# A preactivated 7x7 convolution: banks marked once, merged statistics, a new prologue, and 32 of 128 partitions normalised by GpSimd

## The reference

```
def _gn(v, G=32, eps=1e-05):            # one group per channel
    g = v.reshape(B_, G, C_ // G, H_, W_)
    return ((g - mean(g)) / sqrt(var(g) + eps)).reshape(v.shape)

kern = construct_kernel(weight, P)      # (32, 32, 7, 7): 9 points a channel, bilinear
out  = conv(x_normalised, kern, stride 1, padding 3) + bias
x    = x + out
```

## Time and profile before

| | |
|---|---|
| median of 3 runs | 374.69 us (374.63 to 374.84) |
| profiled execution | 374.54 us, of which its span is 372.7 us |
| PE busy | 330.5 us (89%) |
| DVE busy | 301.7 us (81%) |
| ACT busy | 245.4 us (66%) |
| POOL busy | 99.1 us (27%), nearly all of it the issue of transfers |
| mean granted TensorE clock | 0.954 |

### The profile page before, as it was taken

How to read it: one execution, slowest core, us unless ns; L and a number is a source line. 1 busy time by engine, 2 the same in 40 slices (tenths; PEclk the granted TensorE clock), 3 DMA queues, 4 the chain that set the end, 5 groups by cost and what they waited for, 6 DMA issues and landing times.

```text
span 372.7 us, 9633 instructions
## 1 busy us (share of the span) xinstructions
PE 330.5 (89%) x3426; PEld 206.7 (55%) x3426; DVE 301.7 (81%) x418; ACT 245.4 (66%) x361; POOL 99.1 (27%) x222
## 2 busy tenths in 40 slices
PE   2811799999999999999999999999999999999990
PEld 2600455666656665666655665666556665656560
DVE  6139599989898988989898989899898989898331
ACT  2297786868586785958585858678695858380110
POOL 6002405041424232240504142423224050415000
PEclk9965599999999999999999999999999999999996
DMA  8832608989899989899998989997999976676704
GB/s 144 147 60 57 181 2 183 182 199 204 187 198 194 204 165 216 152 215 173 204 194 189 200 175 197 179 217 150 210 165 215 161 185 138 158 168 164 163 1 86
DMA packets 128424, 61.30 MB, mean 164 GB/s; under 512 B 122228, under 2 KB 122260, under 8 KB 128404
## 3 DMA queue, kind: packets, MB, share of 16 engines
q1 hardware_dynamic: 117108, 25.34, 42.3%
q0 software_dynamic: 9216, 35.30, 41.6%
q10 hardware_dynamic: 2080, 0.40, 0.6%
HBM read 12.88 MB, written 12.85 MB: 69 GB/s over the span
## 4 chain that ended last, share of the span: by engine, by line
PE 60%; DVE 12%; issue 10%; ACT 1%; DVEq 0%
PE ps_s L713 19%; PE ps_x L713 18%; PE ps_eo L713 17%; DVE part L451 4%; DVE xs L447 3%; PE ps_y L696 2%; PE ps_x L696 2%; PE ps_y L713 2%; DVE result L451 2%; PE ps_stat L665 1%; ACT std L297 1%; DVE rtmp L420 1%; DVE rinv L414 1%; DVE scale L425 1%; DVE rtmp L418 1%
## 5 line engine op out<-in xcount | busy, mean ns | idle before, releaser
L642 POOL DMA_DIRECT2D xb<-xs x192 | 92.9, 491 | 244.0 <-ACT xs L322 129.7
L713 PE MATMUL ps_s<-xs,w 128*64 128x392 f16 (+1 forms) x576 | 108.6, 339 | 7.2 <-DVE part L451 5.9
L713 PE MATMUL ps_s<-xb,w 128*64 128x392 f16 (+1 forms) x576 | 108.4, 339 | 6.3 <-DMA xb<-xs 6.3
L713 PEld LDWEIGHTS ps_s<-xs,w 128*64 128x64 f16 x576 | 61.9, 111 | 37.7 <-issue 10.4
L309 ACT ACTIVATE xn<-xraw,offset,scale 96x784 f32<-96x784 f32 x64 | 67.2, 1049 | 19.6 <-DVE offset L427 18.3
L713 PE MATMUL ps_x<-xs,w 128*64 128x392 f16 x384 | 71.2, 342 | 0.0
L713 PE MATMUL ps_x<-xb,w 128*64 128x392 f16 x384 | 71.2, 342 | 0.0
L713 PE MATMUL ps_eo<-xb,w 128*64 128x392 f16 (+1 forms) x384 | 70.7, 342 | 0.0
L713 PE MATMUL ps_eo<-xs,w 128*64 128x392 f16 (+1 forms) x384 | 70.7, 342 | 0.0
L713 PEld LDWEIGHTS ps_s<-xb,w 128*64 128x64 f16 x576 | 61.7, 111 | 8.6 <-DMA xb<-xs 6.7
L713 PEld LDWEIGHTS ps_eo<-xs,w 128*64 128x64 f16 x384 | 41.7, 112 | 27.2 <-issue 6.5
(11 more groups left out here) (87 smaller groups left out, 437.6 us busy)
## 6 DMA issues: line engine op xcount, KB each, us to landing
xb<-xs POOLq DMA_DIRECT2D x96, 180.0 KB, 4.3
xb<-xs POOLq DMA_DIRECT2D x96, 179.0 KB, 4.8
out<-result SPq DMA_DIRECT2D x128, 98.0 KB, 3.4
xraw<-x SPq DMA_DIRECT2D x124, 98.0 KB, 5.8
xraw<-x ACTq DMA_DIRECT2D x4, 98.0 KB, 3.6
wnat<-L_conv_weight SPq DMA_DIRECT2D x1, 36.0 KB, 1.9
pts<-L_conv_P ACTq DMA_DIRECT2D x2, 1.1 KB, 1.9
biascol<-L_conv_bias SPq DMA_DIRECT2D x1, 0.5 KB
```

Of the source, the lines that this page charges most:

```text
L642: pool.dma_start(dst[32 * g:32 * g + 32, 0:run - QP * past], src[32 * f:32 * f + 32, QP * past:run]).then_inc(shifted[par][b], DMA)
L713: last = pe.matmul(into[p:p + HALF, :, :, 0:wide], w[:, n // 2, s, q, t, :], xs_or_xb[:, par, s, n % 2, :, t:t + ROWS, q:q + wide], start= ...
```

## The change

PE no longer zeroes the banks in each unit: eight matmuls of zeros at the start (and two more ahead of unit 0) mark `ps_y` and `ps_x`, and after that no stream into them starts afresh. `seed` waits for the merge that freed the bank instead. The two statistics of a unit share one tile `moments` and one pair of half-width folds per unit, ahead of stream 4 (`both_moments`): variance of unit u+2 and mean of unit u+3. `eo`, `part` and the merges run in the order (column, phase), so that `result` is written with a step of two values and the two banks of a pair are read in turn. DVE's step has a new order: B0, B1, second differences, outs_0, B2, outs_1, var, B3, rstd, mean, B4, outs_2, B5, outs_3, outs_4. ACT's step puts the squares behind B0 and the sums ahead of B2. POOL takes the two normalisations of partitions 96 to 127 over from ACT, ahead of the second third's transfers; DVE and ACT wait for both parts, and so does SP's load. The prologue has another order: POOL issues the transfers of the points and weights, a small identity is built first, the mean of unit 0 is folded within the filter's build, DVE scales the filter, and PE does both statistics of unit 1 (and the mean of unit 2) ahead of unit 0's first stream. The last unit's stores are split over SP and ACT.

```diff
-NORMS = 4
+NORMS = 2
...
-        eo = sb("eo", [128, 2, N], fp32)
-        part = sb("part", [128, 2, 2, N], fp32)
+        eo = sb("eo", [128, N, 2], fp32)
+        part = sb("part", [128, 2, N, 2], fp32)
...
         def two_phases(flat, k):
-            return flat.rearrange("p (n k) -> p k n", k=4)[:, k::2, :]
+            return flat.rearrange("p (n k) -> p n k", k=4)[:, :, k::2]
...
+        def last_store(queue, first):
+            queue.wait_ge(combined, OUTS * UNITS)
+            for m in range(PER):
+                for g in (first, first + 2):
+                    put(queue, UNITS - 1, (UNITS - 1) % 2, m, g)
...
                     sp.wait_ge(seeded, 2 * u + 2)
+                    sp.wait_ge(last_group_normalised, NORMS * u + NORMS)
                     load(u + RING, h)
...  ACT, normalise
-                    for a, b, slot in ((0, 96, 1), (96, 128, 0)):
...
+                    act.activation(xn[0:96, r % 2, SLOTS * m + 1:SLOTS * m + 1 + ROWS, PAD:PAD + SIDE],
...  ACT, step
                 if nxt:
                     high(u + 1, a, *BATCHES[0], first=first)
-                    high(u + 1, a, *BATCHES[1], first=first)
-                middle(u, first)
-                seed(u, h, 0)
                 if stats:
                     squares(u + 2, (h + 2) % RING)
                 if nxt:
+                    high(u + 1, a, *BATCHES[1], first=first)
+                middle(u, first)
+                seed(u, h, 0, first)
+                if early:
+                    sums(u + 3, (h + 3) % RING, nth)
+                if nxt:
                     for batch in BATCHES[2:]:
                         high(u + 1, a, *batch, first=first)
-                seed(u, h, 1)
-                if early:
-                    sums(u + 3, (h + 3) % RING, nth)
+                seed(u, h, 1, first)
...  POOL
+            def normalise(u):
+                pool.wait_ge(newton, NEWTON * (u + 1))
+                if u > 1:
+                    pool.wait_ge(differenced, DIFFS * (u - 1))
+                    pool.wait_ge(hi_ready, NS * (u - 1))
+                    pool.wait_ge(lo_ready, NS * (u - 1))
+                for m in range(PER):
+                    pool.tensor_scalar(xn[96:128, u % 2, SLOTS * m:SLOTS * m + ROWS, PAD:PAD + SIDE],
+                                       image(u % RING, m)[96:128, :].rearrange("p (n w) -> p n w", w=SIDE),
+                                       scale[96:128, m:m + 1], offset[96:128, m:m + 1], ALU.mult, ALU.add
+                                       ).then_inc(last_group_normalised, 1)
...
             for u in range(UNITS):
-                for b in range(THIRDS):
-                    shift(u, u % 2, b)
+                shift(u, u % 2, 0)
+                if u == 0:
+                    shift(u, u % 2, 1)
+                if u + 1 < UNITS:
+                    normalise(u + 1)
+                if u:
+                    shift(u, u % 2, 1)
+                shift(u, u % 2, 2)
...  PE
+            def fold_columns(a, b):
+                for p in (0, HALF):
+                    last = pe.matmul(ps_stat[p:p + HALF, a:b], fold[:, p:p + HALF], moments[:, a:b],
+                                     start=True, stop=True)
+                last.then_inc(folded, 1)
...
-            def start(pair):
-                for k in range(2):
-                    last = pe.matmul(pair[:, k, 0:N], zeros[:, 0:128], zeros[:, 128:128 + N], start=True, stop=False)
-                last.then_inc(started, 1)
...
+            mean(1)
+            both_moments(1)
...
                     if s == 4:
-                        if not first:
-                            pe.wait_ge(combined, OUTS * (u - 1) + 5)
-                        start(ps_y)
+                        if stats:
+                            both_moments(u + 2, early)
                         pe.wait_ge(seeded, 2 * u + 1)
```

More of the change, by code:

```diff
@@ L386, in _ @@
             filter_high(4)
-            high(0, 0, *BATCHES[4], first=True)
-            high(0, 0, *BATCHES[5], first=True)
+            for batch in BATCHES[2:]:
+                high(0, 0, *batch, first=True)
+            squares(1, 1)
+            sums(2, 2, 0)
             root(1)
-            sums(2, 2, 0)
             normalise(1, 1, first=True)
@@ L637, in shift @@
                 dst = xb[:, par, 3 * b:3 * b + 3].rearrange("p s a m n q -> p (s a m n q)")
-                for g in range(GROUPS):
+                for g in (0, 2, 1, 3):
                     past, k = divmod(WINDOW[g] + 2, GROUPS)
@@ L650, in _ @@
         @block.tensor
         def _(pe):
+            pe.wait_ge(zeros_built, 1)
+            for n in range(8):
+                last = pe.matmul(ps_y[:, n % 2, 0:N], zeros[:, 0:128], zeros[:, 0:N], start=True, stop=True)
+            last.then_inc(marked, 1)
             pe.wait_ge(weights_loaded, DMA)
-            pe.wait_ge(eye_built, 2 * GROUPS)
+            pe.wait_ge(ident_built, 2)
             by_point = wnat[:, :].rearrange("o (p k) -> o k p", k=CHUNKS)
             for k in range(CHUNKS):
-                last = pe.matmul(ps_s[0:CP, CH * k:CH * k + CH], by_point[:, k], eye[0:CH, 0:CH], start=True, stop=True)
+                last = pe.matmul(ps_s[0:CP, CH * k:CH * k + CH], by_point[:, k], ident[:, :], start=True, stop=True)
@@ L682, in _ @@
             pe.wait_ge(srow_step, 7)
-            pe.matmul(ps_y[:, 1, 0:3], ones[:, :], srow[:, 2:5], start=True, stop=True).then_inc(scales_in_psum, 1)
-            pe.wait_ge(fold_built, 1)
-            mean(0)
+            pe.matmul(ps_s[:, 128:131], ones[:, :], srow[:, 2:5], start=True, stop=True).then_inc(scales_in_psum, 1)
             variance(0)
-            mean(1)
-            variance(1)
-            pe.wait_ge(zeros_built, 1)
             pe.wait_ge(kern_ready, 2)
             pe.wait_ge(scales_ready, 1)
-            def start(pair):
-                for k in range(2):
-                    last = pe.matmul(pair[:, k, 0:N], zeros[:, 0:128], zeros[:, 128:128 + N], start=True, stop=False)
-                last.then_inc(started, 1)
+            for k in range(2):
+                last = pe.matmul(ps_x[:, k, 0:N], zeros[:, 0:128], zeros[:, 0:N], start=True, stop=True)
+            last.then_inc(marked, 1)
+            mean(1)
+            both_moments(1)
             def convolve(u, par, s, nth):
@@ L743, in _ @@
             for u in range(2):
-                step(u, u, 0, True, first=u == 0)
-            with pe.Fori(1, UNITS // 2 - 1) as it:
+                step(u, u, 0, True, True, first=u == 0)
+            with pe.Fori(1, UNITS // 2 - 2) as it:
                 for h in range(2):
-                    step(it * 2 + h, h, it, True)
-            for h in range(2):
-                step(UNITS - 2 + h, h, UNITS // 2 - 1, False)
+                    step(it * 2 + h, h, it, True, True)
+            for h in range(4):
+                u = UNITS - 4 + h
+                step(u, u % 2, u // 2, u + 2 < UNITS, u + 3 < UNITS)
 def kernel(**inputs):
```

212 lines of the change are left out of this document (119 added, 93 removed).

## The result

The changed kernel takes 335.54 us (335.13 to 337.36, four runs) where the kernel before takes 374.66 (374.50 to 374.84): ratio 0.896, interval 0.893 to 0.899. The forecast was 349 with a range of 344 to 366, so the direction was right and the gain was 39.1 us where 25.7 was forecast. The profiled execution took 337.36 us, the longest of the four, its span 335.5. Against the profiled execution before, unit 1 begins 6.0 us sooner, the 13 units from there to unit 14 take 27.5 less, the last two 2.4 less, and the end 1.2 less.

The account below looks back on a forecast made before the run. PE was taken to bound the unit, DVE close behind. Unit 1's start at 59.3, 13 units of 18.9, 36.0 for the last two, 1.1 and 5.0 at the end, plus 1.84 and 0.15, gave 349 us; range 344 to 366.

Parts of the forecast that it names:

- That leaves 19.73 - 0.86 - 0.31 = 18.56: PE's work per steady unit: 19.73 us less 0.86 of zeroing and 0.31 for one fold leaves 18.56.
- I keep 0.31 for the pair: PE, per unit: the remaining pair of half-width folds costs 0.31 us, with bounds of 0 to 0.62.
- and 0.35 for waits: PE, per unit: 0.35 us of waits, about what PE had before, on top of 18.56, giving 18.9.
- The sum: Whole kernel: 59.3 + 13 x 18.9 + 36.0 + 1.1 + 5.0 = 347.1, plus 1.84 and 0.15: 349 us.
- the forecast 17.3: DVE's work per unit: 18.6 us less 1.3 from faster result writes, with nothing taken for alternate bank reads.
- Rival (b): DVE binds through slow bank reads or result writes: unit up to 20.0 us, kernel 353 to 363; chance 0.12.
- 3.0 was forecast for the two: GpSimd, per unit: two normalising instructions at 1.5 us each, 3.0 together.
- I let DVE pay 0.55 to 1.3: DVE, per unit: waits from GpSimd reading SBUF beside two-input instructions, taken as 0.55 to 1.3 us within 0 to 2.05.
- Rival (c): GpSimd's normalisation bounds the unit if one instruction passes 2.26 us: kernel slower, 377 or up to 401 us; chance 0.08.
- Rival (a): Steady units: loads, ACT's sums, highs and seed close a loop of 20.1 us a unit, kernel 364.5; chance 0.15.
- The first nine microseconds at half the clock stay: Unit 0: PE still runs its first nine microseconds at half the clock; the unit takes 22.9 us instead of 25.04.
- End: After the last unit: outs_4 with its wait 1.1 us, then stores 5.0, four on each queue issued in 2.65.

Follow-up runs that it names:

- e3: The changed kernel with two groups of full-width, one-row matmuls of zeros put back into each unit: 350.44 us, ratio 0.936.
- e4: The changed kernel with the same one-row zeros added to each unit as half-width matmuls: 350.46 us, ratio 0.936.
- e6: The changed kernel with zeros added to each unit as half-width matmuls from all 128 rows: 344.09 us, ratio 0.919.
- e2: The changed kernel with each fold as one full-width matmul instead of two half-width ones: 340.23 us, ratio 0.909.
- e5: The changed kernel with the old layout: result written in steps of four values, banks read one after the other: 340.86 us, ratio 0.914.
- e7: The kernel before with only the zeroing changed: banks marked once, seed waiting for the merge that freed its bank: 360.92 us, ratio 0.963.
- e10: The changed kernel with GpSimd's two normalising instructions replaced by constant writes that read nothing: 346.54 us, ratio 0.921.
- e1: The changed kernel with ACT normalising all partitions again and GpSimd only issuing shifts: 344.34 us, ratio 0.920.
- e13: e10 with two more constant writes by GpSimd into a tile that nobody reads: 335.34 us, ratio 0.897.
- e14: e1 with four constant writes by GpSimd into an unread tile ahead of the second third's shifts: 338.73 us, ratio 0.906.
- e9: The changed kernel with the fold ahead of stream 5 and unit 1's fold behind unit 0's first stream: 339.25 us, ratio 0.902.
- e12: e9 with ACT's sums moved behind two highs and ACT normalising all partitions: 345.71 us, ratio 0.922.
- e18: e9 with SP loading ahead of storing and both seeds early: 336.65 us, ratio 0.900.

## Why the prediction was right and wrong

**What bounds it: right.** PE bounded the unit before and after; the zeroing left its queue and no bank waited for it.

**"That leaves 19.73 - 0.86 - 0.31 = 18.56": the step that failed.** PE's work in a unit is 17.72. The terms were taken from the rows of the removed instructions alone. A zero group costs 0.12 more in the stream behind it (e3, e4; none in e6), 0.24 a unit. A wide fold with a stream behind it costs 0.09 more there (e2); of the two folds before, one had a stream behind it. And "I keep 0.31 for the pair" was 0.06: 0.25. Together 0.58, which leaves 17.98. Of the other 0.26, 0.19 is the stream 0 that no longer starts from a stop; 0.07 stays open.

**"and 0.35 for waits".** In nine of 13 units there was none. The four late ones add 3.8 us in all, 0.29 a unit. So the term was right as a mean, but not for its reason: it was meant as what PE loses in every unit, and it is late loads and late shifts in a few. That the two sizes agree is luck.

**The sum.** Unit 1 begins at 58.16 (forecast 59.3): -1.1. Thirteen units take 234.2, 18.01 each instead of 18.9: -11.5. Units 14 and 15 take 35.3 instead of 36.0: -0.7. From the last matmul to the end it is 7.9 where 1.1 + 5.0 were forecast: +1.8. That is 348.9 - 11.5 = 337.4, the profiled execution's time. The range's lower end stood on P = 18.5. With the lower bound of the fold pair and no waits P would have been 18.25, still too long, since the removed groups had a price from their rows and no bound above it. That bound was the fault of the range.

**DVE: right.** The merges are 1.03 as forecast from the step in the writes, and alternate reading is free (e5). DVE is busy for 16.7 a unit, 0.6 below the forecast 17.3, because that started from 18.6, the unit less two waits; from the busy 18.12 of the earlier trace rows the same 1.3 gives 16.8. Rival (b) fell; but e7 shows how near DVE was: without its own savings the loop through it would have set the unit at 19.3.

**GpSimd: size near, who pays wrong.** 3.0 was forecast for the two, and it is 3.4; one alone takes 1.01. On blocking I let DVE pay 0.55 to 1.3. The timeline above shows 3.38 for the two at 127.26, where they take 2.01 in the prologue: GpSimd waits for B4 and B5, which are 0.59 and 1.09 as ever. In the prologue the payer is DVE: its two additions of two inputs from SBUF take 2.00 beside the reading GpSimd, and 1.29 both in the kernel before and in e10, where GpSimd only writes. This is the lock of the Trainium skill, "SBUF — State Buffer", "Who interferes with whom"; the trace agrees, with e10's unstretched 0.76 for an instruction that reads nothing. That rule of the Trainium skill alone would have let either side pay. In the unit GpSimd paid, which has time, though its record begins 0.02 to 0.07 us ahead of DVE's in all units but one; why it was the one to pay is not shown. The estimate of 1.18 us from the Trainium skill, "GPSIMD Engine Reference", section 3.1, is above the 1.01 measured for an undisturbed one, and the measurement decides. Rival (c) was far off.

**Rival (a)** was at hand: not as the bound of every unit, but as a cause of late ones (the sums' waits for `xraw`), and in e10, and in part in e1, as the cause of a kernel 11 and 9 us slower. What I had not seen is that GpSimd's two instructions hold it off by delaying the shifts.

**Prologue: parts off in both directions.** negmean came at 15.61, not 14.1. The fold sat behind the filter's second chunk, whose matmuls took as long as before, and the weights were turned at 6.26 rather than 5.62, since they are now fetched third in GpSimd's queue. e<-xn started at 23.43 (21.9), 0.7 of it by the blocked additions. Stream 0 started at 37.3 (36.4), behind both_moments(1) as forecast. Unit 0 was shorter than forecast, 20.9 to 22.9. "The first nine microseconds at half the clock stay" is what failed there: the granted clock was 0.50 until 42.16, 4.8 us after stream 0's start, where it had been 9.0 before (39.16 to 48.14). 4.2 us less at half the rate are 2.1 us, the whole miss. What brought the full clock sooner is not shown.

**End.** Four stores on each of two queues take 3.3 us, not 2.65:

```profile
328.71 3.26 SPq L195 DMA_DIRECT2D out<-result  x4
328.71 3.35 ACTq L195 DMA_DIRECT2D out<-result  x4
```

That is 0.82 each where a single queue took 0.66; the rest of the 1.8 is the last store's landing.

**Open.** That a load lands late when the shifts start close behind it is shown by the pairs e10 and e13, e1 and e14; by what mechanism is not: which transfers crowd which in the DMA engines was not measured alone. Which units are late was read in one execution of each kernel. Nor was a version tried in which the shifts go out later without GpSimd being kept busy. DVE's new order, the merged statistics and the prologue were not undone one by one.

## What to carry to other kernels

- The price of an instruction removed from a full PE queue is not only its own row. Compare the stream behind it with a like one that has nothing in front: here a fifth of each zero group's cost (0.12 of 0.55) stood there.
- When a second engine is nearly as full as the first, a cut on the first soon meets it (e7: 1.10 us of PE's work a unit taken away, 0.85 gained). Cut both, and cost the sum as the larger of the two.
- An engine that is off the path may still time the transfers. Before making it faster, ask which transfers start sooner and what they meet: a faster GpSimd step cost 11 us here, and a delay of 3 us, filled with writes that nobody reads, brought back 5.6.
- An engine that starts sooner and stops at the next semaphore has won nothing, and may come out of the stop at half the clock (e9). Look for the next thing it waits for.

## What the runs showed of the hardware

- Going from 128-row half-width matmuls to one-row ones and back costs 0.12 us beside the 0.43 of the group itself, or 0.45 in half width; with 128 rows in half width, the group is 0.33 and the extra is gone (e3, e4, e6).
- A float32 fold of 128 columns of weights is 0.32 + 0.09 us between half-width float16 streams (e2); four half-width matmuls in its place are 0.06.
- A VectorE instruction with two inputs from SBUF and a GpSimd instruction that reads SBUF lengthen each other: beside 0.59 and 1.09 us of such VectorE work GpSimd's 1.01 becomes 1.29 to 1.46 and 1.96 (after), and in the prologue two VectorE additions of 1.29 became 2.00. A GpSimd instruction of the same size that only writes is 0.76 every time (e10).
- A load's median landing is 2.8 or 2.9 us where the shifts start some 4 to 5.5 us behind it (after, e13, e14), 3.8 at 2.6 us (e10), and 4.8 or 5.0 where they start within 1.5 us of it (e12, e1).
- Around a stop of 4 us in unit 0 PE's granted clock fell to 0.50 (1.2 GHz) in e9, from 44.11 to 50.93, and stayed at 1.00 (2.4 GHz) in e18.
- Eight early matmuls of zeros (1.20 to 4.00 us) brought a stretch at the full clock, but not where the filter is built. Engines' busy time and, third from the end, the granted clock, of after:

```profile
4.62:8.03 3.41, 1.12 (x8) 0.94 (x8) 2.01 (x8) 0.79 (x3) 2.46 (x8) 1.00 1.33 209
8.03:14.86 6.83, 6.32 (x15) 5.11 (x16) 2.23 (x6) 1.64 (x4) 4.31 (x8) 0.50 0.94 148
```

Matmuls of the filter's build, of after and then of before:

```profile
12.09 1.91 PE L761 MATMUL ps_eo<-cols,diag 96*128 96x256 f32 x4
15.49 1.13 PE L761 MATMUL ps_eo<-cols,diag 96*128 96x256 f32 x4
```

```profile
11.61 1.91 PE L677 MATMUL ps_eo<-cols,diag 96*128 96x256 f32 x4
14.53 1.03 PE L677 MATMUL ps_eo<-cols,diag 96*128 96x256 f32 x4
```

In after PE was granted 1.00 from 4.62 to 8.03, when it was busy for 1.1 us, and 0.50 from there to 14.86, where four of the matmuls take 1.91; at 1.00, behind 14.86, four take 1.13. In before, PE did nothing until 5.6. Its trace has no record of the clock ahead of 14.01 (the view of a stretch there prints 1.00, which is not a grant), but four matmuls take the same 1.91 before that time and 1.03 after it. So both kernels build the filter at half the clock until about 14 us.
